# Causal small attention: later second sums, a rearranged order of pieces, three masks ahead of the split

## What is computed

```python
q, k, v = x @ Wq.T + bq, x @ Wk.T + bk, x @ Wv.T + bv      # split into 16 heads of 8
q = apply_rope(q) * scale
k = apply_rope(k)
dots = jnp.einsum('bnih,bnjh->bnij', q, k)
mask = i[:, None] < i[None, :]
dots = jnp.where(mask, jnp.float32(-100000.0), dots)
attn = jax.nn.softmax(dots, axis=-1)
o = jnp.einsum('bnij,bnjh->bnih', attn, v)
return o.transpose(0, 2, 1, 3).reshape(b, l, d) @ Wo.T + bo
```

## Time and profile before

| | |
|---|---|
| median of the runs shown | 4903.26 us |
| profiled execution, its own time | 4894.49 us |
| span of its core | 4892.8 us |
| TensorE, busy | 3823.4 us (78%) |
| VectorE, busy | 3405.3 us (70%) |
| ScalarE, busy | 2341.8 us (48%) |
| POOL, busy | 2392.6 us (49%) |
| `l1att`, first and last score | 2183.3 to 2499.6 us |
| `gqa`, first and last score | 3795.0 to 4089.9 us |

### The profile page before, as it was taken

One profiled execution on the slowest core, in us unless ns is written; L12 is line 12 of the kernel. 1 busy time (PEld: TensorE's weight loads), 2 busy tenths in 40 slices (PEclk: granted clock), 3 DMA queues, 4 the chain that ended last, 5 costly groups with the idle time before them and its releaser, 6 DMA issues. The chain is left out here.

```text
span 4892.8 us, 90894 instructions
## 1 busy us (share of the span) xinstructions
PE 3823.4 (78%) x25840; PEld 2727.7 (56%) x25840; DVE 3405.3 (70%) x9524; ACT 2341.8 (48%) x5537; POOL 2392.6 (49%) x3948
## 2 busy tenths in 40 slices
PE   7889797779999799468868947568776887699475
PEld 5666565656666466366656636523332665466365
DVE  7888675556666677556658856669998664588566
ACT  3444464356666466234436634345553454266343
POOL 5666453434444443346644444367776663144443
PEclk9999898789999899689989968879988999899688
DMA  6000232100000133043323311211121331133113
GB/s 236 0 0 1 103 124 85 52 22 1 0 0 0 58 123 113 29 126 109 105 76 120 117 37 54 70 52 62 63 63 55 122 112 42 42 123 115 36 55 86
DMA packets 244547, 341.24 MB, mean 70 GB/s; under 512 B 26976, under 2 KB 187120, under 8 KB 243120
## 3 DMA queue, kind: packets, MB, share of 16 engines
q1 hardware_dynamic: 230960, 309.19, 19.0%
q0 software_dynamic: 13184, 27.22, 1.6%
HBM read 182.77 MB, written 147.26 MB: 67 GB/s over the span
## 5 line engine op out<-in xcount | busy, mean ns | idle before, releaser
L544 DVE TENSOR_REDUCE l0att_rowmax<-l0att_S 128x2 f32<-128x512 f32 x512 | 339.1, 686 | 130.6 <-PE l0att_S L724 128.5
L916 POOL TENSOR_TENSOR wb_prob<-wb_prob,wb_rden 128x128 f32<-128x128 f32 (+1 forms) x512 | 248.9, 508 | 360.7 <-DVE wb_rden L1093 360.2
L544 DVE TENSOR_REDUCE l1ffn_rowmax<-l1ffn_S 128x2 f32<-128x512 f32 x512 | 337.2, 686 | 90.9 <-PE l1ffn_S L724 83.5
L1990 POOL TENSOR_TENSOR ssm_hc<-core_AW_all,ssm_Cs 128x512 f32<-128x512 f32 x256 | 321.1, 1271 | 129.7 <-DVE core_AW_all L2136 96.6
L1455 POOL DMA_INDIRECT results<-e_y,e_back x220 | 210.6, 957 | 304.5 <-DVE e_y L1670 289.5
L958 ACT ACTIVATE wb_prob<-wb_biased,wb_nmax 128x128 f32<-128x128 f32 (+1 forms) x512 | 228.6, 447 | 236.9 <-DVE wb_nmax L1086 234.5
L2235 PE MATMUL ssm_Y<-ssm_hc,core_ident 128*128 128x512 f32 x512 | 288.6, 674 | 56.7 <-POOL ssm_hc L1990 30.5
L2136 DVE TENSOR_TENSOR_SCAN core_AW_all<-core_AW_all,ssm_U 128x512 f32<-128x512 f32 x256 | 310.3, 1212 | 1.1 <-ACT core_AW_all L2079 1.1
L724 PE MATMUL l1ffn_S<-l1ffn_K,l1ffn_Q 128*128 128x512 f32 x512 | 250.2, 492 | 76.9 <-DVE l1ffn_rowmax L544 44.7
L724 PE MATMUL l0att_S<-l0att_K,l0att_Q 128*128 128x512 f32 x512 | 246.8, 485 | 65.6 <-DMA l0att_K<-bounce 51.8
L2079 ACT ACTIVATE core_AW_all<-ssm_dt,ssm_A 128x510 f32<-128x510 f32 x256 | 178.5, 716 | 221.5 <-DVE core_AW_all L2136 219.8
(11 more groups left out here) (498 smaller groups left out, 11451.3 us busy)
## 6 DMA issues: line engine op xcount, KB each, us to landing
bounce<-l0att_parts SPq DMA_DIRECT2D x128, 256.0 KB, 2.8
bounce<-l1ffn_parts SPq DMA_DIRECT2D x128, 256.0 KB, 2.8
ssm_Cs<-c_rows SPq DMA_DIRECT2D x128, 256.0 KB, 3.0
routed<-core_Y SPq DMA_DIRECT2D x8, 2048.0 KB, 24.8
l0att_Q<-bounce SPq DMA_DIRECT2D x128, 128.0 KB
l0att_K<-bounce SPq DMA_DIRECT2D x128, 128.0 KB
bounce<-l1att_parts SPq DMA_DIRECT2D x64, 256.0 KB, 2.8
l1ffn_Q<-bounce SPq DMA_DIRECT2D x128, 128.0 KB
```

Of the source, the lines that this page charges most:

```text
L544: dve.tensor_reduce(out=rowmax[:, jp, qt, 2 * pair:2 * pair + 2], in_=S[a % 2][:].rearrange("p (j k) -> p j k", j=2)[:, :, 0:keys(qt)], op ...
L916: ins = pool.tensor_tensor(out=prob[:, w_ % NP, a:b], in0=prob[:, w_ % NP, a:b], in1=rden[:, w_ % NP, n:n + 1].to_broadcast([P, b - a]), o ...
L1990: pool.tensor_tensor(out=hc[:, u % 4], in0=hs[:, u % 4], in1=Cs[:, n % 4], op=ALU.mult)\
```

## The change

In the causal stages alone, the second half's weighted sum goes from slots 1 and 2 to slots 5 and 6 (`SECOND_AT`), and ScalarE's copy of it from slot 3 to slot 7. The plan of the pieces, used with `rope`, is rearranged: `v` 4 to 7, `n0` and `n1` 5 and 6 to 9 and 10, `h` 7 to 8, `qq` and `kk` 9 and 10 to 12 and 13, `on` 12 to 14, `out` 14 to slot 0 of the round after (its `ahead` is -2), with one more round at the end for it. `mt1` and `mt0` stay at 3 and 11. POOL does masks 8, 9 and 10 ahead of `part(r + 3)`, mask 11 stays behind it. In stages that aren't causal nothing moves.

```diff
         if rope:
-            plan = {3: "mt1", 4: "v", 5: "n0", 6: "n1", 7: "h", 9: "qq", 10: "kk", 11: "mt0", 12: "on", 14: "out"}
+            plan = {0: "out", 3: "mt1", 7: "v", 8: "h", 9: "n0", 10: "n1", 11: "mt0", 12: "qq", 13: "kk", 14: "on"}
...
         ahead = {"h": 3, "qk": 3, "qq": 3, "kk": 3, "v": 2, "mt0": 1, "mt1": 0, "n0": -1, "n1": -1, "on": -1,
-                 "out": -1}
-        ROUNDS = range(-3, SEQS + 1)
+                 "out": -2 if causal else -1}
+        SECOND_AT = 5 if causal else 1
+        ROUNDS = range(-3, SEQS + (2 if causal else 1))
...
-            for r in range(-1, SEQS + 1):
+            for r in range(-1, ROUNDS.stop):
                 hide(r - 1, 12, 15)
...
                 hide(r, 0, 8)
                 if inside(r + 1):
                     part_max(r + 1, 0)
+                hide(r, 8, 11)
                 if inside(r + 3):
                     part(r + 3)
-                hide(r, 8, 12)
+                hide(r, 11, 12)
                 last(r + 3)
...
-                for jp, at in ((1, 3), (0, 13)):
+                for jp, at in ((1, SECOND_AT + 2), (0, 13)):
...
-                    for jp, at in ((1, 1), (0, 10)):
+                    for jp, at in ((1, SECOND_AT), (0, 10)):
```

## The result

The changed kernel took 5013.44 us (median of four runs, 5010.77 to 5020.09), the kernel before 4902.06 on the same chip: a ratio of 1.0231, interval 1.0215 to 1.0247. It is slower by 111 us, where the forecast had 120 us and 5023 us in all, in a range of 4965 to 5065.

The account below looks back on a forecast made before the run. Chains between engines, no full engine: POOL's last mask in `l1att`; key piece, split, store, send, slot 8 in `gqa`. `l1att` +48, `gqa` +67 and start +5 gave +120 us, 5023 us in all, range 4965 to 5065.

Parts of the forecast that it names:

- The chain: Both causal stages: key piece, split, store, send, slot 8, key piece closes the changed round, 22.8 us at full clock.
- The leg from split to slot 8: POOL's split, stores, sends and transfers until slot 8's score: stays at 12.46 us, no part touched.
- The work added from slot 8 to the key piece: On TensorE, pieces, a first-half sum, scores and turns newly ahead of the key piece: 3.66 us a round.
- a sign of the shared chain: Split starts in the changed kernel's trace: 22.8 us apart or more, equal in both stages to about 0.3 us.
- The proof offered for the chain: In `gqa` before the change, legs of 12.46 and 6.68 us make 19.14, against a mean round of 19.15.
- The clock: TensorE after the slot 8 wait: one clock fall a round, 1.48 us, making 24.3; bounds none and 2.96.
- The masks ahead of the split: POOL's masks 8 to 10 ahead of the split cost nothing there; with cover gone, 1.1 us.
- the shadow argument: The wait at `mt1` isn't added to the round: it lies in the shadow of the 12.46 us leg.
- The waits: TensorE idles at least 2 us at `mt1` (1.5 in `gqa`), some 4 at slot 8; none before second sums.
- Start of the stages: Round -1 of both stages: sequence 2's key piece some 2.5 us later, twice, +5 us; bounds 2 and 8.
- Rival C: POOL's chain through `mt1` closes the round, 18.9 us in `l1att`, 18.2 in `gqa`; total 4874 us; chance 0.05.
- The sum on the median: Whole kernel: the worked-out difference, +120 us, added to the median 4903.26 us, not the profiled 4894.49; 5023 us.

Follow-up runs that it names:

- e7: The kernel before with SyncE issuing both sends of the second half ahead of the store in the causal stages; 4905.29 us, ratio 1.0016.
- e5: The changed kernel with SyncE issuing both second-half sends (data and maxima) ahead of the store in the causal stages; 4887.77 us, ratio 0.9975.
- e1: The changed kernel with POOL's masks 8 to 11 all behind the split again; 4982.91 us, ratio 1.0173.
- e11: The changed kernel measured again, nothing altered, against the kernel before; 5010.37 us, ratio 1.0225.
- e2: The changed kernel with query and key pieces back in slots 9 and 10, `n0` and `n1` in 12 and 13; 4925.75 us, ratio 1.0057.
- e6: e5 with the key piece back in slot 10, `n0` and `n1` in 12 and 13; 4911.26 us, ratio 1.0019.

## Why the prediction was right, and where it was off

*The chain.* Right for the changed kernel, with its parts. The leg from split to slot 8 was forecast to stay; it is 11.9 to 12.4 us in all `l1att` rounds and 12.0 to 13.1 in `gqa`. The work added from slot 8 to the key piece was 3.66 us; the leg went from 6.68 to 10.82, 4.1 us. Other `gqa` rounds of the kernel before had up to 7.4, most of them 6.7 to 7.0, so the addition itself holds and the base was a quick round. The spacings came to 23.8 and 24.7 us, from 20.6 and 19.15. They are 0.9 us apart, where the prediction named 0.3 as a sign of the shared chain; the falls of the clock, below, account for that.

*The proof offered for the chain.* This was weaker than it looks. That 12.46 and 6.68 add up to the round shows nothing, for any event between two splits cuts their distance into two such legs; and that the sum met the mean of 19.15 was the choice of the round. Its wait at slot 8, 0.58 us, was the third longest of 13; the mean was 0.3, and seven rounds had 0.15 us or less. In the same `gqa` rounds TensorE waited 1.4 us or more for POOL's last mask in all but the first, and e7 shows that chain closing the round at 18.65 us. Two chains stood within half a microsecond of each other, and the prediction named one. It did little harm: both begin with the key piece, and the later second sums took the other one away. What does show the chain is the wait at slot 8 in every round of the changed kernel, and e5.

*The clock.* Right in kind. Forecast was one fall a round for 1.48 us; the pair of rounds above differs by 12.41 - 10.82 = 1.59. `l1att` rounds with a fall take 24.3 to 24.7 us, where 24.3 was forecast. What was mis-sized is how many there are, in both directions: in `l1att` five of 13 rounds have no fall in the chain (21.9 to 23.1 us), in `gqa` all but the first have one and three of them a longer one (25.6 to 26.2 us). So `l1att` came out at +41 where +48 stood and `gqa` at +72 for +67. That the total of +120 lies so near is in part luck, as these two errors cancel. The `l1att` rounds alternate for a reason that the prediction did not see: when the clock falls after the wait at `mt1`, TensorE reaches slot 8 later, its wait there is 1.7 to 2.1 us instead of 3.1 to 3.4, and in four of those seven rounds the clock then holds. The falls at `mt1` are free, as they lie in covered time.

*The masks ahead of the split.* The step that failed. It said that they cost nothing there. They do not delay the split, and the shadow argument holds for time; but they move 1.1 us of idle time from a covered place to slot 8, where it brings the clock down inside the chain. e1 puts that at some 25 us, which the forecast had inside its one fall a round.

*The waits.* `mt1` was put at 2 us or more and 1.5 in `gqa`; 2.4 and 1.75. Slot 8 at some 4 us; 1.4 to 3.4 and 1.9 to 5.0. The wait ahead of the second sums went, as said. SyncE's store is issued 0.03 us after the split's end, as before (2321.62 + 1.28 against 2322.93 in the trace).

*Start of the stages.* +5 in the sum; from first score to third split it is 12.87 and 12.87 us for 11.52 and 11.34, +2.9. The tails, up to what follows each stage, differ by less than 2 us.

*Rival C* was put at 5% as a statement about this kernel, and it was false here. But its numbers, 18.9 and 18.2 us, became true to within 0.2 us in the rounds of e5 without a fall, once the data chain was out of the way.

*The sum on the median.* The profiled execution of the changed kernel has a span of 5018.4 us, 125.6 more than before; 7.5 of it lie ahead of the first changed stage (its first score starts at 2190.79, not 2183.26), where the instructions are the same. In the profile of e11 that score starts at 2183.20. So that part is no effect of the change.

## What to carry to other kernels

Find the chain that closes a round before moving anything: take one instruction that runs once per round, and follow from it, wait by wait, back to its run in the round before. The legs between two of its runs add up to its spacing whichever events are chosen; a leg belongs to the chain only if its end was waited for, and in every round, so look at all rounds and at the second-latest chain too. An operation inside a leg costs its own duration, once per round, in every round, even while no engine is full; the same operation outside costs nothing. A transfer that waits in a queue behind another one inherits all that the other waits for, so the order on the queue that issues DMAs is part of the schedule. And idle time is not all alike: where it lies decides whether a drop of TensorE's clock falls into the chain.

## What the runs showed of the hardware

The granted clock fell to half after waits of less than 3 us too. In the kernel before it fell after ten of the 13 waits of 2.1 to 2.6 us ahead of `l1att`'s second sums, and after none of the 13 of 1.4 to 1.8 us in `gqa`. In `l1att` of the changed kernel it fell after all five waits of 3.1 us or more at slot 8 and after three of the seven between 1.6 and 2.2 us; a fall cost the chain 1.2 to 1.7 us. The length of the wait does not settle it alone: one `l1att` wait of 3.51 us at `mt1` in e1 left the clock up.

The store and the send move at different rates. Three windows of the `gqa` stage of the kernel before, during the store, during the send, and after it (last two columns DMA share and GB/s):

```profile
3963.00:3963.50 0.50, 0.11 (x1) 0.00 (x0) 0.34 (x1) 0.35 (x1) 0.50 (x4) 1.00 1.00 326
3968.50:3969.00 0.50, 0.50 (x4) 0.32 (x3) 0.50 (x3) 0.50 (x2) 0.00 (x0) 1.00 0.26 107
3971.50:3972.00 0.50, 0.43 (x3) 0.23 (x3) 0.50 (x2) 0.50 (x2) 0.30 (x1) 1.00 0.00 0
```

The send's four transfers of 128 KB use a quarter of the DMA engines' time and run at some 100 GB/s, so 512 KB take 5 us, where the store's 1 MB took some 3 at 330 GB/s. That is the larger part of the 8.74 us from send to score. A layout of the send that keeps all engines busy should shorten that leg, which counts where the transfer is waited for (the changed kernel, e2, e6); it wasn't tried.
